# Sums of squared queries in two fp32r passes split by GpSimd, and a new order of the copies, in a fused cross-attention and expert kernel

## The reference, cut to what matters

```python
def rms_norm(x, scale, eps=EPS):
    ms = jnp.mean(jnp.square(x), axis=-1, keepdims=True)
    return x * jax.lax.rsqrt(ms + eps) * scale
...
q = rms_norm(x @ q_w + q_b, nq_s).reshape(B, S, H, D)      # mean over all 16 * 128 = 2048 columns
k_txt = rms_norm(txt_ctx @ k_w + k_b, nkt_s).reshape(B, -1, H, D)
...
scores = jnp.einsum('bshd,blhd->bhsl', q, k) * scale
```

## Time and profile before

| | |
|---|---|
| median of 3 runs | 1920.23 us (1919.83 to 1922.81) |
| the profiled execution | 1918.63 us, its span 1916.8 us |
| mean granted TensorE clock | 0.973 of full speed |
| busy share of the span: PE, PEld, DVE, ACT, POOL | 91%, 80%, 73%, 51%, 60% |
| `project`'s steady loop, heads 0 to 12 | 69.4 to 217.1 us of the span |

### The profile page before, as it was taken

The page is one execution under the profiler, slowest core; times in us unless marked ns, Lnnn a source line. Parts: engine busy times, 40 slices in busy tenths (PEclk is TensorE's granted clock), DMA queues, the critical chain, the costliest instruction groups (busy, mean ns, idle before and its releaser), DMA issues. The chain is left out here.

```text
span 1916.8 us, 30691 instructions
## 1 busy us (share of the span) xinstructions
PE 1751.0 (91%) x8731; PEld 1534.5 (80%) x8731; DVE 1397.1 (73%) x2577; ACT 983.2 (51%) x1657; POOL 1149.5 (60%) x989
## 2 busy tenths in 40 slices
PE   7899979999999999999999999999992998699998
PEld 6566669889888888888898898888892886688887
DVE  4344477887978878878878879788782564577776
ACT  3444445555655655555555556556552553244443
POOL 1000278888788788788788887887862331133332
PEclk9999999999999999999999999999996999799999
DMA  3365564465564665554564665556436782133332
GB/s 110 121 208 197 194 183 111 107 116 123 123 120 114 130 121 117 122 135 114 116 132 108 116 126 125 116 116 131 98 90 195 252 274 92 66 107 115 116 109 78
DMA packets 417364, 251.19 MB, mean 131 GB/s; under 512 B 350272, under 2 KB 368832, under 8 KB 415520
## 3 DMA queue, kind: packets, MB, share of 16 engines
q1 hardware_dynamic: 417312, 250.55, 51.2%
HBM read 187.71 MB, written 60.10 MB: 129 GB/s over the span
## 5 line engine op out<-in xcount | busy, mean ns | idle before, releaser
L1322 ACT ACTIVATE p_high<-psum,key_rms 128x448 fp32r<-128x448 f32 x384 | 244.7, 637 | 397.1 <-PE psum L1145 397.0
L1143 PE MATMUL psum<-p_high,c_high 128*128 128x448 f32 (+1 forms) x768 | 287.8, 375 | 48.0 <-DVE p_low L1405 48.0
L1405 DVE TENSOR_TENSOR p_low<-psum,p_high 128x448 fp32r<-128x448 f32 x384 | 236.4, 616 | 100.2 <-ACT psum L1324 99.1
L1143 PE MATMUL psum<-u_high,c_high 128*128 128x448 f32 x768 | 285.5, 372 | 21.0 <-DVE psum L1416 15.1
L1144 PE MATMUL psum<-u_low,c_high 128*128 128x448 f32 x768 | 282.5, 368 | 0.0
L1145 PE MATMUL psum<-u_high,c_low 128*128 128x448 f32 x768 | 281.5, 366 | 0.0
L1145 PE MATMUL psum<-p_high,c_low 128*128 128x448 f32 (+1 forms) x768 | 281.5, 366 | 0.0
L1144 PE MATMUL psum<-p_low,c_high 128*128 128x448 f32 (+1 forms) x768 | 281.0, 366 | 0.0
L1416 DVE COPY psum<-beta_wide 128x448 f32<-128x448 f32 x416 | 259.4, 627 | 20.2 <-DMA beta_wide<-absorbed_biases 4.4
L1617 POOL TENSOR_TENSOR c_low<-stage,c_high 128x512 fp32r<-128x512 f32 x208 | 273.6, 1316 | 0.0
L1324 ACT ACTIVATE psum<-psum,key_rms 128x448 f32<-128x448 f32 x384 | 232.3, 605 | 0.0
(11 more groups left out here) (241 smaller groups left out, 4018.3 us busy)
## 6 DMA issues: line engine op xcount, KB each, us to landing
stage<-in_ctx SPq DMA_DIRECT2D x210, 256.0 KB, 2.8
averages<-o_raw SPq DMA_DIRECT2D x64, 448.0 KB, 5.2
o_stage<-averages SPq DMA_DIRECT2D x32, 896.0 KB, 5.4
u_raw<-absorbed_queries SPq DMA_DIRECT2D x60, 448.0 KB, 5.5
absorbed_queries<-u_stage SPq DMA_DIRECT2D x14, 1792.0 KB, 6.8
beta_wide<-absorbed_biases SPq DMA_DIRECT2D x32, 448.0 KB, 5.3
recip_wide<-reciprocals SPq DMA_DIRECT2D x32, 448.0 KB, 4.1
p_wide<-probs_by_expert SPq DMA_DIRECT2D x32, 448.0 KB, 3.6
```

The lines of the kernel that those rows point to most:

```text
L1143: nc.tensor.matmul(out, high, rhigh, start=start, stop=False, **kw)
L1322: nc.scalar.activation(p_high[:, probs_slot(u), :], src, ACT.Exp, scale=key_rms[:, t:t + 1])
L1405: return nc.vector.tensor_tensor(out, a, b, ALU.subtract)
```

## The change: what it does

- **Squares in two passes.** `square_w` becomes fp32r. `q_square` has one buffer in place of two, and GpSimd splits it: a cast to `square_high` (fp32r), and, after a wait for that cast, a subtraction into `square_low` (fp32r). TensorE multiplies each half by both parts: 4 fp32r matmuls for each head in place of 2 fp32 ones, and it waits for GpSimd's `square_split` where it waited for ScalarE's `q_taken`.
- **Waits.** ScalarE's `take(h)` waits, half by half and ahead of `q_high`, for GpSimd's split of head h - 1, and no longer for TensorE's sums of head h - 2. GpSimd, from head 1 on, waits before each cast for TensorE's squares of the same half one head before. `first_low` comes in GpSimd's queue behind the split of the last head.
- **Order of the copies.** For heads 0 to 13, ScalarE and VectorE copy blocks 0 and 1 of u right after `take(h + 2)`, then split the weights, then copy blocks 2 and 3. Before, the weights came first and then all four blocks.

```diff
-                square_w = sb("square_w", [P, H, 1 + 2 * H], stack=proj)
+                square_w = sb("square_w", [P, H, 1 + 2 * H], F32R, proj)
...
-            nc.gpsimd.memset(square_w[:, :, :], 0.0).then_inc(square_w_zero, 1)
+            nc.gpsimd.memset(square_w[:, :, :].bitcast(F32), 0.0).then_inc(square_w_zero, 1)
...
-        q_square = sb("q_square", [P, 2, N])
+        q_square = sb("q_square", [P, N])
+        square_high, square_low = sb("square_high", [P, N], F32R), sb("square_low", [P, N], F32R)
...
+        square_high_ready, square_split = sem("square_high_ready"), sem("square_split")
...
             def squares(h):
                 for half in range(2):
-                    pe.wait_ge(q_taken, 2 * h + half + 1)
-                    nc.tensor.matmul(psum[0:ROWS_SQ, SUMS + half, 0:HALF], square_w[:, h, :],
-                                     q_square[:, h % 2, cols(half)], start=h == 0, stop=h == H - 1)\
-                        .then_inc(squares_summed, 1)
+                    pe.wait_ge(square_split, 2 * h + half + 1)
+                    out = psum[0:ROWS_SQ, SUMS + half, 0:HALF]
+                    nc.tensor.matmul(out, square_w[:, h, :], square_high[:, cols(half)], start=h == 0, stop=False)
+                    nc.tensor.matmul(out, square_w[:, h, :], square_low[:, cols(half)], start=False,
+                                     stop=h == H - 1).then_inc(squares_summed, 1)
...
-                if h >= 2:
-                    act.wait_ge(squares_summed, 2 * (h - 1))
                 for half in range(2):
                     unit = ("q", h, half)
+                    if h >= 1:
+                        act.wait_ge(square_split, 2 * (h - 1) + half + 1)
                     act.wait_ge(q_done, done(unit))
                     src = psum[:, bank[unit], 0:HALF]
                     nc.scalar.activation(q_high[:, h % QRING, cols(half)], src, ACT.Identity, bias=bias)
-                    nc.scalar.activation(q_square[:, h % 2, cols(half)], src, ACT.Square, bias=bias)\
+                    nc.scalar.activation(q_square[:, cols(half)], src, ACT.Square, bias=bias)\
                         .then_inc(q_taken, 1)
...
             for h in range(H):
                 if h + 2 < H:
                     take(h + 2)
+                if h < H - 2:
+                    copy_u(h, range(2))
                 if h + 1 < H:
                     weights_k(h + 1)
                 if h + 3 < H:
                     weights_q(h + 3)
-                copy_u(h, range(4) if h != H - 2 else range(3))
+                copy_u(h, range(2, 4) if h < H - 2 else range(3) if h == H - 2 else range(4))
...
             for h in range(H):
                 if h + 2 < H:
                     take(h + 2)
+                if h < H - 2:
+                    copy_u(h, range(2))
                 if h + 1 < H:
                     weights_k(h + 1)
...
                 if h < H - 2:
-                    copy_u(h, range(4))
+                    copy_u(h, range(2, 4))
...
         def gpsimd(gp):
-            first_tiles[5](gp)
+            for h in range(H):
+                for half in range(2):
+                    n = 2 * h + half
+                    square, high = q_square[:, cols(half)], square_high[:, cols(half)]
+                    gp.wait_ge(q_taken, n + 1)
+                    if h >= 1:
+                        gp.wait_ge(squares_summed, n - 1)
+                    nc.gpsimd.tensor_copy(high, square).then_inc(square_high_ready, 1)
+                    gp.wait_ge(square_high_ready, n + 1)
+                    nc.gpsimd.tensor_tensor(square_low[:, cols(half)], square, high.bitcast(F32), ALU.subtract)\
+                        .then_inc(square_split, 1)
+                if h == H - 1:
+                    first_tiles[5](gp)
```

## The result

| | before | changed |
|---|---|---|
| median on the first chip | 1921.3 us (4 runs) | 1901.37 us (4 runs, 1898.59 to 1905.13) |
| ratio, 95% interval | | 0.9897 [0.9874, 0.9921] |
| the profiled execution, its span | 1918.6, 1916.8 us | 1903.7, 1902.0 us |
| the same kernel on a second chip | 1920.69 us (11 runs) | 1903.28 us (4 runs), ratio 0.9911 [0.9896, 0.9925] |

The forecast was 1902, in a range from 1897 to 1911. The changed kernel is 1% faster.

What follows compares the result with a forecast made beforehand. TensorE bounds the kernel, busy 10.98 of a head's 11.3 us. Heads of 9.98 for 11.36 us save 17.9 over 13; start costs 0.1, end gains 0.3: about 18 us less, median 1902, range 1897 to 1911.

Steps and rivals of the forecast that it cites:

- Squares, 0.80 a head: TensorE's squares: four fp32r passes of 0.205 us, 0.82 in place of 1.62, 0.80 us less in each head.
- Copies, 0.6 a head: u blocks: copying ahead of the weight splits removes both TensorE stalls at block 2, 0.6 us a head.
- The entry of the squares: A 0.1 us TensorE stall just before the squares, kept in the forecast head of 9.98 us.
- ScalarE's waits, 0.05: ScalarE's new waits ahead of q_high for GpSimd's split: charged 0.05 us a head (nothing to 0.1).
- GpSimd: GpSimd's split: cast about 0.56, subtraction 1.13 us; half 1 done at T+6.3 (T: head's first query matmul), hidden from TensorE.
- The rival of a late GpSimd: Rival, 4 in 100: split pairs over 3.5 us make TensorE wait before the squares; slower, about 1929 us.
- The lock of the Trainium skill: VectorE's two-SBUF-operand weight splits and GpSimd block each other; could take most of GpSimd's 1.5 us room, sum unchanged.
- q_low held by GpSimd: Rival, 7 in 100: GpSimd's subtraction blocks VectorE's q_low, block 1, half 1 starts 0.65 us later each head; about 1910.
- Start: First heads: GpSimd's four splits lie on the path and the 1.6 us saved on squares is lost; 0.1 us slower.
- End: Last pass before the flip: a ScalarE and VectorE chain limits it; flip about T+12.3 for T+12.56, gain 0.3 us.
- The rest at nothing: Everything after the stage is moved earlier as a whole, costed at nothing.

Runs made afterwards that it cites:

- copies_only: Kernel before with only the new order of the copies, fp32 squares kept: 1910.48 us, ratio 0.9952 to before.
- gp_once: Changed kernel plus one more GpSimd subtraction into a spare tile, for half 0 of each head: 1903.67 us, ratio 0.9908 to the kernel before.
- gp_twice: Changed kernel plus one more GpSimd subtraction into a spare tile for both halves of each head: 1918.10 us, ratio 0.9985 to the kernel before.
- bias_moved: Changed kernel with head h + 1's six bias matmuls behind u block 0 of head h, and at the start head 1's squares behind head 2's queries: 1893.33 us.
- squares_only: Changed kernel with the old order of the copies on both engines, two-pass squares and GpSimd's split kept: 1927.75 us, ratio 1.0043 to the kernel before.
- gp_beside_old: Kernel before (fp32 squares, old order) plus GpSimd's cast and subtraction into tiles nobody reads: 1938.21 us, ratio 1.0091 to before.

## Why the prediction was right, and where it was not

- **Squares, 0.80 a head:** 0.82 us for four passes; the 33 columns cost nothing.
- **Copies, 0.6 a head:** both stalls of block 2 went; copies_only gave 0.66.
- **The entry of the squares:** its 0.1 went too (97.12 to 97.32), though I kept it in the sum. The head is 9.84, not 9.98: 19.7 us in 13 heads for 17.9.
- **ScalarE's waits, 0.05:** block 1, half 1 starts at T+4.66 for T+4.61.
- **GpSimd:** casts 0.56, subtractions 1.16 for 1.13, half 1 split at T+6.3 as worked out. gp_once confirms that one more subtraction stays hidden, though it too meets wk_low. The rival of a late GpSimd is real, but its place and its point were off. I had the loop free of cost up to 2.5 us a pair and no loss before 3.5; gp_twice, at 2.9, lost 0.76 us in each of 13 heads, 10 us, and with its start nearly the whole gain. The step that failed is that a late GpSimd was priced by TensorE's wait alone and not by the weight splits that it would meet: they stretched its two last subtractions by 0.39 us, about half of the 0.76.
- **The lock of the Trainium skill:** I let the sum stand by it, since the weights come after T+6.2. That is right for this change, but only by its new order. What I didn't see is that the reorder is what makes the split affordable, by taking the first copies out from behind wk_low: with the two steps in separate hands, the sum of parts (0.8 for one, 0.6 for the other) is wrong by 1.05 us a head.
- **q_low held by GpSimd:** no; 0.68 us as before.
- **Start:** 12.72 us from the first queries to those of head 2 for 12.53, 0.2 more (0.1 forecast). **End:** T+12.29 for T+12.56, the 0.3 forecast.
- **The rest at nothing:** right in the medians of the first chip (19.9 less, 19.8 of it in front of the flip), not in those of the second (17.4 less) nor in the two profiles, where 4.7 and 2.4 us came back, the larger part of the 4.7 with the clock. The sum has no term for the clock. That the median fell within 1 us of 1902 is in part luck: the way to the flip gained 1.7 more than forecast, and the kernel before stood at 1921.3, 1.1 above the figure that the sum was taken from.

## What to carry to other kernels

Work given to an idle GpSimd stretches VectorE's instructions that read two SBUF operands (wk_low, 0.87 to 1.78 us and more), and not those that read one (q_low stayed at 0.68). It costs time when something that TensorE waits for stands behind the stretched instruction. So go through what VectorE does in just those microseconds and what stands behind it, and move the awaited copies ahead of its two-operand instructions first. An edit of two parts can work though one of them alone loses; test each alone before dropping either. A stall of TensorE on a bank can be filled with independent matmuls: bias_moved took out the whole of the one that the reorder had left.

## What was not expected of the hardware

- A GpSimd subtraction that nobody waits for made a head 1.05 us longer, 11.36 to 12.41; in the other order it cost nothing, and the two kernels stand at 1938 and 1909 us. In gp_once the same overlap, in the new order, cost nothing either.
- A wait of TensorE of 1.1 to 1.25 us, inside heads in which it is busy for some 90% of the time, was followed by a stretch at the lower clock sometimes and not always: in squares_only and in gp_beside_old in two heads of 13 each, at 1.5 us a time, and behind the flip in five profiles of seven.
- In gp_twice and squares_only the instructions of both engines stretched, GpSimd's by 0.05 to 0.23 us, VectorE's by 0.9 to 1.04 us.
